# Stacking five chunks of a tile through PE and ACT, field by field, in a DLRM tower kernel

## The chip, the cores and the metric

The kernel runs on one core of one Trainium2 chip. The time is the device time of one execution in microseconds; the figure for a kernel is the median of its runs. The profile is of one further execution, and "the span" is its time from the first to the last instruction.

## The reference

2048 samples have 39 categorical features and 16 dense ones. Each feature f has a table with 1,000 to 125,000 rows of 32 numbers. All 741 pairs of features interact through a 32 x 32 matrix per pair, and a small MLP follows:

```
e = stack([tbl_f[ids[:, f]] for f in range(39)])          # 2048 x 39 x 32
z[b, p] = sum_ac e[b, i, c] * w[a, p, c] * e[b, j, a]      # p runs over pairs i < j
h = relu(concat([z, dense]) @ W_top1 + b_top1)             # 757 -> 512
h = relu(h @ W_top2 + b_top2)                              # 512 -> 256
y = h @ W_top3                                             # 256 -> 1
```

## The kernel before, in words

**Tiles, chunks, units, batches.** The samples are cut into 4 tiles of 512 (`NT`, `NB`). Four features form a chunk g (0 to 9; chunk 9 has three fields), so that 4 x 32 numbers fill the 128 partitions. A unit (g, gi, j) is the product of feature j of chunk g with the up to four features of chunk gi. There are 200 units in a tile, in the order of `UNITS`, which takes the chunks as `PHASES = (0, 1, 2, 3, 7, 4, 8, 5, 6, 9)`. Two units are a step, two steps a batch; a tile is 50 batches. Chunk (t, g) means chunk g of tile t.

**A unit.** `interact` (L578) multiplies on PE the pair matrices (`w4`, stationary) with the stacked form of feature j (`e4`, moving, 512 samples) into one of two buffers of `u_ps`. `multiply` (L907) on DVE multiplies a step of `u_ps` with the transposed embeddings `eT` into `prod`. `reduce` (L604) on PE sums over the 32 numbers into `z_ps`, for the batch before. ACT copies finished tiles of `z_ps` to `zT` (`take_z`, L781). In a batch PE runs, in this order: two calls of `interact`, pieces of the MLP of the tile before, `reduce`, `turn` of a chunk, `look_up`s, and, in tile 0, `make_half`. PE, DVE, ACT, POOL and SP each have a program of their own with a fixed order and wait on semaphores.

**Where the embeddings come from.** POOL gathers rows of large tables with an indirect DMA of 128 rows at a time (L422), 4 for each field; the first 96 gathers, which are tile 0's, wait until the third gather before has landed (`WINDOW`), the later ones until DVE has reached a step (`s_mul`). The buffer `e_rows` holds four chunks. `turn` (L528) transposes a gathered chunk into `t_ps` on PE. Small tables are kept in SBUF in three bf16 parts, and `look_up` (L543) multiplies them with one-hot matrices made by DVE (`one_hot_slice`, L886). `FIRST_TILE` and `OTHER_TILES` give the batches in which a chunk is turned or its slices looked up; a chunk's last such batch is its `COMPLETE` batch.

**From `t_ps` to `e4`.** `take_chunk` (L707) on ACT copies `t_ps` to the high part in `parts` (fp32r) and to `eT`; `split_chunk` (L863) on DVE writes the low part. `e4` wants for each field high and low values in alternating partitions, and every field spread over all 128. Most chunks go through DRAM: SP stores both parts (`store_parts`, L461) and loads them again (`stack_chunk`, L471) into `e4`, two loads of 512 KB. Five chunks of tile 0, those in `MADE`, are stacked by PE instead: `make_half` (L562) multiplies the 32 partitions of a field with `rep`, high and low part accumulated, for two fields into two banks, and `take_half` (L727) on ACT copies both into `e4`. For the last three of them the banks are `m_ps`, which the MLP uses from tile 1 on, and the second bank of `z_ps`. `e4` has four slots (`E4_SLOT`); `parts` has two buffers.

**Weights.** In tile 0 the pair matrices are split as well, in 13 preparations k of 16 units: ACT loads them (`load_weights`), casts the high part (`weights_high`, L747), DVE subtracts (`weights_low`, L871), ACT stores both (`weights_rest`), and SP brings pieces to `w4` (`bring_piece`). `PREPS` gives the batch of preparation k: 4 to 12 are in batches 6, 9, 13, 17, 21, 25, 29, 33 and 37. In a batch's program on ACT `weights_high` stands behind `take_z`, `take_chunk` and `take_half`; on DVE `weights_low` stands behind the one-hots.

**First uses in tile 0.** Chunk 4 is first used in batch 14, chunk 8 in the middle of batch 19, chunk 5 in batch 28, chunk 6 in batch 36, chunk 9 in batch 42. They are complete in batches 7, 13, 19, 28 and 31.

Of the kernel before, what the change touches and what calls it, by code (L numbers as in the profile page):

```python
# [5 lines left out]
P = 128  # L6
F = 39
D = 32
# [13 lines left out]
def fields_in(g):  # L22
    return min(C, F - C * g)
# [101 lines left out]
E4_SLOT = {0: 0, 1: 2, 2: 3, 3: 1, 7: 2, 8: 3, 4: 0, 5: 1, 6: 0, 9: 1}  # L125
# [25 lines left out]

MADE = ((0, 1), (0, 0), (0, 2), (0, 3), (0, 7))
MADE_FIRST = 2
MADE_IN = {1: (((0, 2), 0), ((0, 2), 1)), 4: (((0, 3), 0), ((0, 3), 1)), 5: (((0, 7), 0),), 6: (((0, 7), 1),)}
MLP_WEIGHTS_BATCH = 7
LATE = (17, 39)
# [8 lines left out]
ORDER = [(0, g) for g in BEGIN] + [(t + nxt, g) for t in range(NT) for g, nxt, turn, slices in chunks_of_tile(t)]  # L165
POS = {c: n for n, c in enumerate(ORDER)}
# [22 lines left out]

def stores_to(n):  # L190

    return len([m for m in range(n + 1) if (m - n) % 2 == 0 and ORDER[m] not in MADE])


def halves_before(c, half):
# [5 lines left out]
def e4_before(c):  # L201

    t, g = c
    same = [x for x in PHASES if E4_SLOT[x] == E4_SLOT[g]]
    n = same.index(g)
    return (t, same[n - 1]) if n else (t - 1, same[-1]) if t else None


def e4_loads(c):

    same = [x for x in PHASES if E4_SLOT[x] == E4_SLOT[c[1]]]
    return len(same) * c[0] + same.index(c[1]) + 1
# [5 lines left out]
for t in range(NT):  # L218
    for g, nxt, turn, slices in chunks_of_tile(t):
        c = (t + nxt, g)  # L220
# [9 lines left out]
    INDICES.setdefault(LAST_SLICE.get(LOOKED[LPOS[c] - 2], -1) + 1, []).append(c)  # L230
for b, cs in COMPLETE.items():
    for c in cs:
        if c in MADE:
            continue
        x = e4_before(c)
        free = NBAT * x[0] + J_LAST[x[1]] // UPB + 1 if x else 0

        late = LATE[0] <= b < LATE[1]
        STORES.setdefault(b + 1 + late, []).append(c)
        STACKS.setdefault(max(b + (4 if late else 3 if b < LATE[0] else 2), free), []).append(c)  # L240
# [43 lines left out]
def tower(nc, tables, ids, hot_ids, hot_rows, dense, w, w1, b1, w2, b2, w3, sel_in, ident_in, y):  # L284
# [4 lines left out]
    with ExitStack() as ctx:  # L289
# [9 lines left out]
        parts = sb("parts", [P, 2, 2, NB], F32R)  # L299
        e4 = sb("e4", [P, ES, C, NB], F32R)  # L300
# [98 lines left out]
        def step_after(t, g):  # L399

            return NS * t + J_LAST[g] // UPS + 1
# [117 lines left out]
        def _(pe):  # L519
# [42 lines left out]
            def make_half(c, half):  # L562
# [12 lines left out]
                                                start=h == 0, stop=h == 1)  # L575
                last.then_inc(s_stk, 1)

            def interact(t, n):  # L578
                s = NS * t + n
                if s >= 2:  # L580
                    pe.wait_ge(s_mul, s - 1)
                slots = [e_slot(t, UNITS[UPS * n + i][1]) for i in range(UPS)]
                for i in range(UPS):
                    u = UPS * n + i
                    g, gi, j = UNITS[u]
                    if u == J_FIRST[g]:
                        pe.wait_ge(s_e4[E4_SLOT[g]], 32 * e4_loads((t, g)))
                    if u % PW == 0:
                        p = NPW * t + u // PW
                        pe.wait_ge(s_w4[p % WR], 16 * (p // WR + 1))  # L590
                    place = i if slots[0] <= slots[1] else 1 - i
                    p = NPW * t + u // PW
                    last = nc.tensor.matmul(u_ps[:, s % 2, place, :], w4[:, p % WR, (u % PW) * P:(u % PW + 1) * P],  # L593
                                            e4[:, E4_SLOT[g], j - C * g, :], start=True, stop=True)
                last.then_inc(s_u, 1)
# [86 lines left out]
            for t in range(NT):  # L682
                for b in range(NBAT):
                    for x in range(SPB):
                        interact(t, SPB * b + x)
                    if t:
                        for piece in mlp_pieces(b, t == NT - 1):
                            mlp_piece(t - 1, *piece)
                    if b:
                        reduce(t, b - 1)  # L690
                    elif t:
                        reduce(t - 1, NBAT - 1)
                    for c in TURNS.get(NBAT * t + b, ()):
                        turn(c)
                    for c, k in TAKES.get(NBAT * t + b, ()):
                        look_up(c, k)
                    if t == 0:
                        for c, half in MADE_IN.get(b, ()):
                            make_half(c, half)
                    if t == NT - 1:  # L700
                        for m, k in EARLY.get(b, ()):
                            early_piece(t, m, k)
# [3 lines left out]
        def _(act):  # L706
            def take_chunk(c):  # L707
                t, g = c
                n = POS[c]
                rows = D * fields_in(g)  # L710
                if n >= 2:
                    if ORDER[n - 2] in MADE:
                        act.wait_ge(s_stk, 2 * MADE.index(ORDER[n - 2]) + 2)
                    else:
                        act.wait_ge(s_scr[n % 2], 32 * stores_to(n - 2))
                if hot(c):
                    act.wait_ge(s_look, LOOK_BEFORE[c] + slices_of(g))
                else:
                    act.wait_ge(s_tp, GPOS[c] + 1)
                nc.scalar.copy(parts[0:rows, n % 2, 0, :], t_ps[0:rows, :]).then_inc(s_eh, 1)  # L720

                before = t - 2 if g in TWO_PLACES else t - 1
                if before >= 0:
                    act.wait_ge(s_mul, NS * (before + 1))
                nc.scalar.copy(eT[0:rows, e_slot(t, g), :], t_ps[0:rows, :]).then_inc(s_et, 1)  # L725

            def take_half(c, half):  # L727
                made = MADE.index(c)
                act.wait_ge(s_stk, 2 * made + half + 1)
                x = e4_before(c)  # L730
                if x:
                    act.wait_ge(s_u, step_after(*x))
                slot, q = E4_SLOT[c[1]], UPS * half
                if made < MADE_FIRST:
                    nc.scalar.copy(e4[:, slot, q:q + UPS, :], u_ps[:, half, :, :]).then_inc(s_e4[slot], 16)
                else:
                    nc.scalar.copy(e4[:, slot, q, :], m_ps[:, :]).then_inc(s_e4[slot], 8)
                    nc.scalar.copy(e4[:, slot, q + 1, :], z_ps[:, 1, :]).then_inc(s_e4[slot], 8)

            def load_weights(k):  # L740
                a, b = PREP_UNITS[k]
# [44 lines left out]
            def take_mlp(t, layer, m, src):  # L786
                act.wait_ge(s_m, NI * t + ITEM[layer, m] + 1)
                if layer == 1:
                    if m == 0 and t > 0:
                        act.wait_ge(s_y, 16 * t)  # L790
                    nc.scalar.activation(h1[:, m, :], src, ACT.Relu, bias=b1s[:, m:m + 1]).then_inc(s_mc, 1)  # L791
                elif layer == 2:
                    nc.scalar.activation(h2[:, t % 2, m, :], src, ACT.Relu, bias=b2s[:, m:m + 1]).then_inc(s_mc, 1)
                else:
                    nc.scalar.copy(y_sb, src[0:1, :]).then_inc(s_mc, 1)
                    act.wait_ge(s_mc, NI * (t + 1))
                    act.dma_start(y[t:t + 1, :], y_sb).then_inc(s_y, 16)
# [30 lines left out]
            for t in range(NT):  # L828
                for b in range(NBAT):
                    if t:  # L830
                        for layer, m, k in mlp_pieces(b, t == NT - 1):
                            if k == LAYER_INPUTS[layer] - 1:
                                take_mlp(t - 1, layer, m, m_ps[:, :])
                    for tile in range(NZ):
                        done = ends_tile(tile) // UPB + 1
                        if done == b:
                            take_z(t, tile)
                        elif t and done == NBAT and b == 0:
                            take_z(t - 1, tile)
                    for c in COMPLETE.get(NBAT * t + b, ()):  # L840
                        take_chunk(c)
                    if t == 0:
                        for c, half in MADE_IN.get(b, ()):
                            take_half(c, half)
                        if b == LAST_TABLE_BATCH:
                            table_high(HOT_CHUNKS[-1])
                        if b == LAST_TABLE_BATCH + 2:
                            table_middle(HOT_CHUNKS[-1])
                        if b - 1 in PREPS:
                            weights_rest(PREPS[b - 1])  # L850
                        if b in PREPS:
                            weights_high(PREPS[b])
                        if b in PREP_LOADS:
                            load_weights(PREP_LOADS[b])
# [171 lines left out]
```

## Time and profile before

| | |
|---|---|
| median of 3 runs | 739.4 us (738.17 to 740.45) |
| profiled execution | 739.08 us |
| its span | 737.2 us, mean granted TensorE clock 0.977 |
| PE busy | 678.2 us |
| DVE busy | 608.3 us |
| POOL busy | 415.6 us |
| ACT busy | 104.3 us |
| moved by DMA | 141.40 MB |

The engines' busy times overlap in time. PEld are PE's weight loads. In timelines a row is a run of like instructions: its start in us from the span's start, its length in us, engine, line, operation, tiles and shapes, count, and in brackets the idle time of the engine before it with what ended it. A name with a q (SPq, ACTq) is the engine's queue, which issues DMAs.

### The profile page before, as it was taken

What the parts mean: (1) busy time and instruction counts of PE and PEld (TensorE: products, weight loads), DVE (VectorE), ACT (ScalarE), POOL (GpSimd) and SP (SyncE); (2) the same over time, 40 slices, a digit from 0 to 9 for tenths busy, and PEclk for the clock granted to TensorE, in tenths of its full rate; (3) what the DMA queues carried; (4) which work ended last, traced back from release to release, by engine and by line L of the source; (5) the groups of instructions that cost most, each with busy time, mean ns of one, the idle gap of its engine ahead of it and who ended that gap; (6) DMA issues with size and microseconds to landing.
All of it is one profiled execution on the core that took longest, in us unless ns stands there. A gap on an engine that the chain in (4) does not pass through costs nothing.

```text
span 737.2 us, 10924 instructions
## 1 busy us (share of the span) xinstructions
PE 678.2 (92%) x4202; PEld 274.6 (37%) x4202; DVE 608.3 (83%) x773; ACT 104.3 (14%) x186; POOL 415.6 (56%) x424
## 2 busy tenths in 40 slices
PE   0678886898997999999999999999999999999998
PEld 0233332333333444434344444433434444343443
DVE  3776797799996998898889997998889978788740
ACT  3423301111110010101211010110110101011002
POOL 5777465567777766567766665567766666000000
PEclk9888999899998999999999999999999999999999
DMA  7644979779876573547675582728686373553200
GB/s 200 209 119 138 334 272 301 252 231 314 284 227 202 195 257 108 166 140 236 224 225 192 202 281 68 240 85 259 194 270 214 125 254 98 179 174 104 97 0 0
DMA packets 72271, 141.40 MB, mean 192 GB/s; under 512 B 13829, under 2 KB 23704, under 8 KB 72092
## 3 DMA queue, kind: packets, MB, share of 16 engines
q1 hardware_dynamic: 48796, 116.86, 46.2%
q10 hardware_dynamic: 9984, 16.94, 6.4%
q0 software_dynamic: 13440, 6.91, 6.4%
q8 instruction: 33, 0.54, 0.3%
q14 instruction: 18, 0.15, 0.1%
HBM read 109.66 MB, written 31.00 MB: 191 GB/s over the span
## 4 chain that ended last, share of the span: by engine, by line
PE 70%; DVE 14%; issue 7%; DMA 4%; POOL 3%; ACT 1%; SPq 0%; DVEq 0%; ACTq 0%
PE u_ps L593 23%; PE z_ps L617 21%; DVE prod L914 9%; PE m_ps L630 8%; PE t_ps L556 7%; DVE one_hot L902 4%; POOL e_rows L422 3%; PE m_ps L632 3%; PE t_ps L537 2%; DMA e<-scratch 1%; DMA e_rows<-in_tbl_dram,idx 1%; PE u_ps L652 1%; PE u_ps L661 1%; PE m_ps L634 1%; PE t_ps L644 1%
## 5 line engine op out<-in xcount | busy, mean ns | idle before, releaser
L422 POOL DMA_INDIRECT e_rows<-in_tbl_dram,idx x420 | 415.4, 989 | 212.9 <-issue 89.9
L914 DVE TENSOR_TENSOR prod<-u_ps,eT 128x1024 f32<-128x1024 f32 x400 | 469.5, 1216 | 77.6 <-PE u_ps L593 77.1
L593 PE MATMUL u_ps<-e,w 128*128 128x512 f32 x800 | 260.9, 437 | 24.6 <-DVE prod L914 14.6
L617 PE MATMUL z_ps<-prod,sel 128*32 128x512 f32 x1600 | 222.9, 614 | 0.0
L593 PEld LDWEIGHTS u_ps<-e,w 128*128 128x128 f32 x800 | 132.2, 190 | 173.4 <-DVE prod L914 85.9
L902 DVE TENSOR_SCALAR one_hot<-hot_idx,row 125x512 bf16<-125x512 f16 (+2 forms) x296 | 107.6, 420 | 9.6 <-PE t_ps L556 5.8
L556 PE MATMUL t_ps<-one_hot,tb 125*32 125x512 bf16 x1344 | 104.2, 392 | 10.5 <-DVE one_hot L902 9.1
L556 PEld LDWEIGHTS t_ps<-one_hot,tb 125*32 125x32 bf16 x1344 | 43.7, 99 | 89.3 <-issue 57.6
L617 PEld LDWEIGHTS z_ps<-prod,sel 128*32 128x32 f32 x1600 | 33.8, 108 | 111.7 <-issue 87.4
L630 PE MATMUL m_ps<-zT,w1s 128*128 128x512 f32 x144 | 73.5, 592 | 0.0
L720 ACT CAST parts<-t_ps 128x512 fp32r<-128x512 f32 (+1 forms) x40 | 23.4, 586 | 295.4 <-PE t_ps L556 162.4
L868 DVE TENSOR_TENSOR parts<-eT,parts 128x512 fp32r<-128x512 f32 (+1 forms) x40 | 27.3, 683 | 3.2 <-ACT eT L725 3.2
L630 PEld LDWEIGHTS m_ps<-zT,w1s 128*128 128x128 f32 x144 | 27.2, 189 | 6.4
L791 ACT ACTIVATE h<-m_ps,b1s 128x512 f32<-128x512 f32 x13 | 9.0, 689 | 145.1 <-PE m_ps L630 143.9
L784 ACT COPY zT<-z_ps 128x512 f32<-128x512 f32 x24 | 14.1, 586 | 102.9 <-PE z_ps L617 102.9
L537 PE MATMUL t_ps<-ident,e_rows 128*128 128x128 f32 (+2 forms) x112 | 19.2, 296 | 6.6 <-DMA e_rows<-in_tbl_dram,idx 6.6
L632 PE MATMUL m_ps<-h,w2s 128*128 128x512 f32 x48 | 24.5, 592 | 0.0
L725 ACT COPY eT<-t_ps 128x512 f32<-128x512 f32 (+1 forms) x40 | 23.7, 591 | 0.0
L537 PEld LDWEIGHTS t_ps<-ident,e_rows 128*128 128x128 f32 (+2 forms) x112 | 12.2, 142 | 30.3 <-issue 27.1
L875 DVE TENSOR_TENSOR h<-h 128x512 fp32r<-128x512 f32 (+1 forms) x13 | 8.7, 668 | 2.7 <-ACT h L751 2.7
L751 ACT CAST h<-h 128x512 fp32r<-128x512 f32 (+1 forms) x13 | 7.9, 609 | 17.2 <-DMA h<-in_w_dram 17.2
L632 PEld LDWEIGHTS m_ps<-h,w2s 128*128 128x128 f32 x48 | 9.0, 188 | 2.1
(52 smaller groups left out, 122.2 us busy)
## 6 DMA issues: line engine op xcount, KB each, us to landing
w<-w_rows SPq DMA_DIRECT2D x100, 512.0 KB
e<-scratch SPq DMA_DIRECT2D x62, 512.0 KB, 5.7
scratch<-parts SPq DMA_DIRECT2D x62, 256.0 KB
w_rows<-h ACTq DMA_DIRECT2D x48, 256.0 KB
e_rows<-in_tbl_dram,idx POOLq DMA_INDIRECT x420
hot_idx<-hot SPq DMA_DIRECT2D x12, 512.0 KB
h<-in_w_dram ACTq DMA_DIRECT2D x12, 256.0 KB, 4.3
e<-scratch SPq DMA_DIRECT2D x8, 384.0 KB
```

Source lines behind the costliest of these rows:

```text
L422: pool.indirect_dma_start(e_rows[:, r, n, D * q:D * q + D], None, tables[f], bass.IndirectOffsetOnAxis(ap=idx[:, t, f * TPG + n:f * TPG + ...
L537: last = nc.tensor.transpose(t_ps[0:hi, b * P:b * P + P], rows, ident[:, :])
L556: last = nc.tensor.matmul(t_ps[D * q:D * q + D, :], tb[0:HP, part, col:col + D], one_hot[0:HP, n % OS, here * NB:(here + 1) * NB], start=k ...
L593: last = nc.tensor.matmul(u_ps[:, s % 2, place, :], w4[:, p % WR, (u % PW) * P:(u % PW + 1) * P], e4[:, E4_SLOT[g], j - C * g, :], start=T ...
L617: last = nc.tensor.matmul(z_ps[D * quad:D * quad + D, z % 2, :], sel[:, D - 1 - row:2 * D - 1 - row], prod[:, (NS * t + n) % PR, place, :] ...
L630: last = nc.tensor.matmul(m_ps[:, :], w1s[:, k, m * P:m * P + P], zT[:, t % 2, k, :], start=k == 0, stop=stop)
L632: last = nc.tensor.matmul(m_ps[:, :], w2s[:, k, m * P:m * P + P], h1[:, k, :], start=k == 0, stop=stop)
L720: nc.scalar.copy(parts[0:rows, n % 2, 0, :], t_ps[0:rows, :]).then_inc(s_eh, 1)
L725: nc.scalar.copy(eT[0:rows, e_slot(t, g), :], t_ps[0:rows, :]).then_inc(s_et, 1)
L868: nc.vector.tensor_tensor(parts[0:rows, n % 2, 1, :], eT[0:rows, e_slot(t, g), :], parts[0:rows, n % 2, 0, :].bitcast(F32), ALU.subtract). ...
L902: last = nc.vector.tensor_scalar(one_hot[0:HP, n % OS, i * NB:(i + run) * NB], hot_idx[0:HP, LPOS[c] % 2, x * NB:(x + run) * NB], (row10 i ...
L914: nc.vector.tensor_tensor(prod[:, s % PR, :, :], u_ps[:, s % 2, :, :], e, ALU.mult).then_inc(s_mul, 1)
```

## The change

Chunks 4, 8, 5, 6 and 9 of tile 0 are no longer stored and loaded. `FIELD_WISE` gives each its first batch. At the end of PE's batch `first + q` `make_field` multiplies field q's high and low part (two matmuls, accumulated) into the one bank `m_ps`, and `take_field` on ACT copies it into `e4`. `take_field` stands in ACT's batch ahead of `take_z`, `take_chunk` and the weights. A field's matmuls wait until the field before has been copied out of `m_ps`. `take_chunk` waits for the last field that was made from its buffer of `parts`, in place of a store.

```diff
+FIELD_WISE = {(0, 4): 9, (0, 8): 15, (0, 5): 21, (0, 6): 30, (0, 9): 35}
+STACKED = MADE + tuple(FIELD_WISE)
...
-    return len([m for m in range(n + 1) if (m - n) % 2 == 0 and ORDER[m] not in MADE])
+    return len([m for m in range(n + 1) if (m - n) % 2 == 0 and ORDER[m] not in STACKED])
+
+
+def stk_at(c, part):
+
+    earlier = STACKED[:STACKED.index(c)]
+    return sum(2 if x in MADE else fields_in(x[1]) for x in earlier) + part + 1
+
+
+def stk_after(c):
+    return stk_at(c, (2 if c in MADE else fields_in(c[1])) - 1)
+
+
+def field_in(b):
+
+    return [(c, b - first) for c, first in FIELD_WISE.items() if first <= b < first + fields_in(c[1])]
...
-        if c in MADE:
+        if c in STACKED:
             continue
...
+            def make_field(c, q):
+
+                n = POS[c]
+                pe.wait_ge(s_el, n + 1)
+                d = c if q else STACKED[STACKED.index(c) - 1]
+                pe.wait_ge(s_e4[E4_SLOT[d[1]]], 32 * e4_loads(d) - (32 - 8 * q if q else 0))
+                own = slice(D * q, D * q + D)
+                for h in range(2):
+                    last = nc.tensor.matmul(m_ps[:, :], rep[own, 2 - 2 * h:2 - 2 * h + P], parts[own, n % 2, h, :],
+                                            start=h == 0, stop=h == 1)
+                last.then_inc(s_stk, 1)
...
+                    if t == 0:
+                        for c, q in field_in(b):
+                            make_field(c, q)
...
-                    if ORDER[n - 2] in MADE:
-                        act.wait_ge(s_stk, 2 * MADE.index(ORDER[n - 2]) + 2)
+                    if ORDER[n - 2] in STACKED:
+                        act.wait_ge(s_stk, stk_after(ORDER[n - 2]))
...
+            def take_field(c, q):
+                act.wait_ge(s_stk, stk_at(c, q))
+                act.wait_ge(s_u, step_after(*e4_before(c)))
+                slot = E4_SLOT[c[1]]
+                rest = 8 if q < fields_in(c[1]) - 1 else 32 - 8 * q
+                nc.scalar.copy(e4[:, slot, q, :], m_ps[:, :]).then_inc(s_e4[slot], rest)
...
+                    if t == 0:
+                        for c, q in field_in(b):
+                            take_field(c, q)
                     for tile in range(NZ):
```

## Rows read from the trace of the kernel before

**Rows 1.** The page's busy line: us, share of the span, instructions.

```profile
PE 678.2 (92%) x4202; PEld 274.6 (37%) x4202; DVE 608.3 (83%) x773; ACT 104.3 (14%) x186; POOL 415.6 (56%) x424
```

**Rows 2.** Waits of PE from 70 to 300 us: total, times, longest.

```profile
PE u_ps L593 <- DVE prod L914: 12.1, 29, 1.3
PE u_ps L593 <- DMA e<-scratch: 5.8, 1, 5.8
PE t_ps L537 <- DMA e_rows<-in_tbl_dram,idx: 4.1, 1, 4.1
```

**Rows 3.** Timeline of PE around batch 19.

```profile
131.03 1.19 PE L593 MATMUL u_ps<-e,w 128*128 128x512 f32 x2 [5.76 <-DMA e<-scratch]
...
134.50 1.18 PE L593 MATMUL u_ps<-e,w 128*128 128x512 f32 x4
```

**Rows 4.** The chain that ended last, 60 to 300 us: start, us, what.

```profile
115.66 3.91 DMA scratch<-parts
...
120.27 10.62 DMA e<-scratch
```

**Rows 5.** Timeline of PE at `make_half`; tile `e`, its copies on ACT (min/median/max ns).

```profile
81.98 0.50 PE L574 MATMUL m_ps<-parts,rep 32*128 32x512 f32 x1
...
82.65 1.19 PE L593 MATMUL u_ps<-e,w 128*128 128x512 f32 x4
...
L737 ACT CAST e<-m_ps x4: 585/586/587, 72.6 to 82.8; 128x512 fp32r<-128x512 f32 x4
```

**Rows 6.** Timelines of ACT, PE and DVE, batches 16 to 19.

```profile
116.64 0.62 ACT L751 CAST h<-h 128x512 fp32r<-128x512 f32 x1 [4.60 <-DMA h<-in_w_dram]
...
120.88 1.06 PE L617 MATMUL z_ps<-prod,sel 128*32 128x512 f32 x8
...
122.66 0.68 DVE L875 TENSOR_TENSOR h<-h 128x512 fp32r<-128x512 f32 x1
...
123.26 3.48 DVE L914 TENSOR_TENSOR prod<-u_ps,eT 128x1024 f32<-128x1024 f32 x3
```

**Rows 7.** Timeline of DVE behind batch 13.

```profile
112.08 0.69 DVE L875 TENSOR_TENSOR h<-h 128x512 fp32r<-128x512 f32 x1 [1.22 <-ACT h L751]
```

**Rows 8.** Timelines of PE and DVE, start of batch 25.

```profile
151.76 1.61 PE L593 MATMUL u_ps<-e,w 128*128 128x512 f32 x4
...
154.52 2.34 DVE L914 TENSOR_TENSOR prod<-u_ps,eT 128x1024 f32<-128x1024 f32 x2
```

**Rows 9.** Timelines of DVE, ACT and PE, batch 33 and batches 37 and 38.

```profile
183.23 0.68 DVE L875 TENSOR_TENSOR h<-h 128x512 fp32r<-128x512 f32 x1
...
194.89 0.58 ACT L784 COPY zT<-z_ps 128x512 f32<-128x512 f32 x1 [19.06 <-PE z_ps L617]
195.37 0.41 ACT L751 CAST h<-h 128x256 fp32r<-128x256 f32 x1
195.41 1.20 PE L593 MATMUL u_ps<-e,w 128*128 128x512 f32 x4
...
195.81 0.43 DVE L875 TENSOR_TENSOR h<-h 128x256 fp32r<-128x256 f32 x1
```

**Rows 10.** Timelines of POOL and PE, batches 48 to 50.

```profile
221.44 0.73 PE L593 MATMUL u_ps<-e,w 128*128 128x512 f32 x2
...
221.96 0.94 POOL L422 DMA_INDIRECT e_rows<-in_tbl_dram,idx  x1 [0.30 <-issue]
...
228.96 2.05 PE L593 MATMUL u_ps<-e,w 128*128 128x512 f32 x4
...
232.81 1.35 PE L593 MATMUL u_ps<-e,w 128*128 128x512 f32 x4
```

**Rows 11.** POOL's waits from 87.6 to 160 us; two stretches (PE, PEld, DVE, ACT, POOL busy; clock; DMA share, GB/s).

```profile
POOL e_rows L422 <- DMA e_rows<-in_tbl_dram,idx: 26.5, 18, 3.2
...
107.00:117.00 10.00, 8.12 (x49) 2.76 (x47) 8.78 (x11) 1.95 (x4) 7.86 (x8) 1.00 0.50 155
117.00:127.00 10.00, 7.67 (x38) 2.38 (x38) 9.52 (x9) 0.26 (x1) 4.10 (x5) 1.00 1.01 322
```

More of the change, by code:

```diff
@@ L728, in take_half @@
                 made = MADE.index(c)
-                act.wait_ge(s_stk, 2 * made + half + 1)
+                act.wait_ge(s_stk, stk_at(c, half))
                 x = e4_before(c)
```

## The prediction

> **What bounds the kernel now.** I read the busy line of the page first [rows 1]: PE is busy for 92% of the span and DVE for 83%, ACT for 14%. Work added to ACT is nearly free, work added to PE or DVE may not be. Then I read what PE waits for between 70 and 300 us [rows 2]: one wait of 5.8 us for the load of `e` from scratch, and one of 4.1 us for gathered rows. Nearly everything else it waits for is DVE, in pieces up to 1.3 us. The change takes away the first wait and may touch the second; both lie in tile 0. A batch is two calls of `interact` (2 x 2 matmuls of L593), so the n-th batch starts at matmul 4n of L593; I counted batches that way in the timeline.
>
> The timeline of PE shows the first wait [rows 3]. It is in the middle of batch 19, at the first unit of chunk 8: after 5.76 us without work the next matmuls start at 131.03. The chain of waits shows the two transfers that the change removes for this chunk, 3.91 us of store and 10.62 us of load [rows 4].
>
> **What it removes.** Without the load the second pair of batch 19 waits for the product before it. The three products in a row from 123.26 us [rows 6] take 1.16 us each; the second ends at 125.6. So the pair starts at 125.6 and not at 131.03, 5.4 us earlier. After the wait PE ran slow: from 131.03 to batch 20 at 134.50 is 3.47 us [rows 3], and in the same work at full clock a pair is 0.7, `reduce` 1.0 and `turn` 0.4, with gaps 2.3 us. That is 1.2 us more. Batch 20 would start at 127.9: **6.6 us** earlier, before anything is paid.
>
> The other four chunks cost PE no wait today; removing their 4 stores and loads gains nothing by itself on PE. All five together are 5 x 0.5 MB stored and 5 x 1 MB loaded less on the DMA engines (0.75 of it for chunk 9).
>
> **What it adds.** 19 fields (4+4+4+4+3), each two matmuls on PE and one copy on ACT. The nearest row is `make_half`, which issues four such matmuls: from its start at 81.98 to the next `interact` at 82.65 are 0.67 us [rows 5]. Its four run two on two, the pairs on different row groups and banks. A field's two have one row group and one bank, one after the other, so a field costs as long as a half: 0.65 us. Bounds: 0.34 (half of that, if a neighbour overlaps it), and 1.0 where the clock is low. The 19 fields are 12.4 us of PE. The copy is 0.59 us of ACT [rows 5], 11 us in all, on an engine with 633 us idle.
>
> The Trainium skill (TensorEngine Tiling (Array Packing), Key Properties and Gotcha 1: PSUM Pressure) says that tiles in different row groups run in parallel and need different PSUM banks. It speaks against stacking field by field through one bank: packed in pairs the 19 fields would be 6.3 us of PE, unpacked they are 12.4. The two-on-two starts in the trace agree with it.
>
> How much lies on the path differs by batch, so I laid the fields into the timeline chunk by chunk, moving each instruction to what it waits for.
>
> Chunk 4 (batches 9 to 12): batches 9 to 12 have two slices of look-ups each, so DVE makes one-hots between its products and is the later engine. Only the last field pushes the look-ups of batch 13, whose end already releases ACT and through it a waiting `weights_low` (1.22 us, [rows 7]). Cost 0.5 us; bounds 0 and 1.3.
>
> Chunk 8 (batches 15 to 18): lean batches without one-hots, where PE and DVE take turns. `reduce` of batch 17 starts at 120.88 [rows 6] and the next `interact` follows it at once. The field goes there. In batch 16 it delays the next product by 0.6 us net. In batch 17 there is more: `weights_high(7)` is behind `take_field` in ACT's program, and ran far ahead before (done at 117.3, [rows 6]). Now it waits for the field: PE's field ends about 1.7 us after `reduce` starts, copy 0.6, cast 0.6, and `weights_low(7)`, which DVE reached at 122.66 [rows 6], waits some 1.4 us. That is the wait [rows 7] shows for `take_chunk`. Behind it stand all DVE products, and PE behind these; on ACT the stores of the split weights and the next raw load stand behind the copies too, and SP's pieces of `w4` behind those, but what is prepared in batch 17 is first used in batch 28, so these have some 30 us to spare. SP only loses waits: its pieces of `w4` stood behind stores and stacks, and are paced by `s_u` anyway. Sum for chunk 8: 2.5 us; bounds 1.0 and 4.3. The last field is copied about 0.6 us before the second pair of batch 19 needs it.
>
> So batch 20 starts at 127.9 + 0.5 + 2.5 = 130.9 and not 134.50: 3.6 us earlier.
>
> Chunk 5 (batches 21 to 24): a field ends the batch while DVE makes the next one-hots. After batch 24 PE could start at 151.76, DVE wants its result at 154.52 [rows 8]; 0.65 us more disappears. Cost 0, bounds 0 and 1.3. If that cover were gone it would be 2.6.
>
> Chunks 6 and 9 (batches 30 to 33, 35 to 37): PE has waits for DVE to spare up to batch 31 and few after. In batch 33 `weights_high(11)` is behind `take_field`; with the look-ups before it the cast ends near 184.3, DVE wants it at 183.23 [rows 9]: 1.1 us. Batches 35 and 36 each have look-ups and a field: PE becomes the later one, 0.7 us. In batch 37 the field ends at 195.41 + 0.65 if nothing is late; then `take_field`, `take_z` (0.58) and `weights_high(12)` (0.41) follow in ACT's order, before `weights_low(12)`, which ran at 195.81 [rows 9]. That is 1.7 us, partly the same lateness. Sum **3.5 us**; bounds 1.9 (PE work added less its slack there) and 6.5.
>
> The main line therefore reaches batch 40 with 6.6 - 0.5 - 2.5 - 0 - 3.5 = 0.1 us gained: about as before.
>
> **The second wait.** At the end of batch 48 `turn` of chunk (1, 3) waits 4.1 us [rows 2] for its last gather, which POOL runs at 221.96 and which lands six us later [rows 10]. The clock then falls: batch 48 takes 7.5 us (221.44 to 228.96) where 3.1 would do, batch 49 takes 3.85 (to 232.81) where 2.5 would. Together 4.4 + 1.35 = **5.8 us**. Why is that gather late? POOL issues one every 1.25 us without rest from 160 us on, so its lateness is from before. The first 96 gathers wait each for the landing of the third before, and from 87.6 us, where the first removed store has just been issued, to 160 us such waits are 26.5 us in 18 pieces, 21 us above the ordinary 0.3 us [rows 11]; the first of them (3.2 us) still belongs to loads issued before, so 18 us stand to be changed. Where the DMA engines are half idle (107 to 117, share 0.50) POOL does not wait; at share 1.01 (117 to 127) it does, 5.6 us [rows 11]. Chunks 4, 8 and 5 store and load 4.5 MB in this time, and the two stretches shown move 1.6 and 3.2 MB in 10 us each; at their mean rate of 0.24 MB per us the 72 us hold 17 MB, so a quarter of the traffic goes, in bursts. I take 8 us of them as gone; bounds 2 and 13. With the main line at its old time, 4.1 us suffice to end the wait. From batch 50 on PE runs without idle time to the end (in steady tiles only DVE waits), so what is gained here stays.
>
> **Sum.** Against the profiled execution's 739.1 us (span 737.2 and 1.9 around it): 0.1 + 5.8 = 5.9 us less, 733.2. The median of the runs is 0.3 us above that execution: 733.5 us.
>
> **Rivals.**
> A. *The gather stays late.* The first wait moves to the second: main line gains, turn (1, 3) waits until 228 as before. It speaks for it that POOL is at its rate of 1.25 us from 160 us on, so nothing later can make up; against it that its waits follow the DMA share. POOL earlier by 0 to 2 us gives 737 to 739.4, no change.
> The Trainium skill (DMA: Bandwidth & Descriptors, Queues, rings and completion order) says that each DMA engine takes turns between its queues by packets. By that rule a gather is slowed by other queues having work at all, not by how much, and a shorter queue of SP helps only where it runs empty; the quiet stretch at share 0.50 fits it as well. Its time is that of A.
> B. *The fields are cheap.* DVE hides most of them, as its full stretches suggest: main line costs 3 us in place of 6.5, gain 3.6 there, and POOL early by over 8 us: 729.9. If POOL is only 6 earlier, 732.
> C. *PE becomes the bound from batch 9 to 37*, the other side. All 19 fields on the path at 0.65 are 12.4 us, and the casts behind `take_field` add 1.4 + 1.1 + 1.7 = 4.2. Against 6.6 + 5.8 gained: 4.2 us slower, 743.6. It decides from 12.4 us of cost on, that is from every field paid in full. Against it: PE has 12.1 us of waits for DVE between 70 and 300 us [rows 2], most of them in these batches, and half of the fields lie in batches with one-hots.
> D. *The change does nothing for the first wait*, since the last field of chunk 8 is taken late by ACT: needs ACT blocked by a weight load for over 3 us in batches 17 and 18. These loads are now issued later too, but four batches ahead of use. 737.
>
> **How the numbers follow.** About 0.3% (2.2 us) is what a measurement of this kernel can tell from none. Forecast (gain 3 to 8 us, around 733.5) 0.55; A 0.15, of which a third at the edge counts as faster; B 0.16; C 0.10; D 0.04. Faster by over 0.3%: 0.55 + 0.16 + 0.05 = 0.76, less 0.02 for sizes: 0.74. Within: 0.10 + 0.04 = 0.15 with these. Slower: 0.11. The range leaves out C and the far end of B: low 729.0 (B with its bound), high 739.5 (A at nothing).
>
> **What would show it.** In the profile after: no wait of PE for `e<-scratch` in tile 0; make_field's matmuls 0.33 us apart and its copies 0.59 us; batch 20 near 131 us at full clock; waits of DVE for ACT's L751 cast in batches 17, 33 and 37, of 1 to 2 us; batch 40 near 200 us as before; POOL's waits for landings between 87.6 and 160 us about 18 us in place of 26.5; no wait of `turn` near 222 us and the clock at 1.00 from 80 us on. I am wrong if POOL is not earlier (batch 49 still starts near 229), or if PE's batches 15 to 37 grow by over 0.6 us each.

## The result and the profile after

The changed kernel takes 736.1 us, median of 20 runs (730.32 to 739.01), against 738.29 us (734.78 to 741.08) for the kernel before in 20 runs on the same chip. The ratio is 0.9957 [0.9937, 0.9976], that is 3.2 us less [1.8, 4.7]. The two medians alone differ by 2.2 us; the ratio is taken over all the runs, and gains are given by it below. The forecast was 5.9 us less. The sign and the range hold, the size is about half.

One thing was misread, in the description of the change as well as in the prediction: the fields do not stand at the end of PE's batch. In the changed kernel the call of `make_field` stands right behind the two `interact`s, ahead of the MLP's pieces, `reduce`, `turn` and `look_up`. Experiment e4 below builds the place that was assumed.

The page of the changed kernel, its busy line (us, share of the span, instructions) and what the queues moved; its span is 734.3 us, the execution 736.1 us, the mean granted clock 0.977:

```profile
PE 690.1 (94%) x4240; PEld 282.0 (38%) x4240; DVE 608.0 (83%) x773; ACT 115.1 (16%) x205; POOL 414.0 (56%) x424
...
DMA packets 68304, 133.94 MB, mean 182 GB/s; under 512 B 13509, under 2 KB 23384, under 8 KB 68124
```

Against [rows 1]: 38 more matmuls and 19 more copies, 11.9 us more of PE and 10.8 of ACT, 7.5 MB less. PE's share grew by two points and the kernel still got faster.

The waits of PE from 70 to 300 us (total, times, longest), to be read against [rows 2], then those of POOL from 87.6 to 160 us, against [rows 11], and of DVE from 70 to 230 us:

```profile
PE u_ps L623 <- DVE prod L957: 7.7, 17, 1.5
PE m_ps L592 <- ACT e L771: 1.3, 1, 1.3
...
POOL e_rows L440 <- DMA e_rows<-in_tbl_dram,idx: 14.1, 12, 2.8
...
DVE h L918 <- ACT h L791: 5.4, 4, 2.9
```

The waits for `e<-scratch` (5.8 us) and for gathered rows (4.1 us) are both gone. POOL's landing waits fell from 26.5 to 14.1 us. Neither gives its full length at the end, as the starts of the batches show (us from the span's start):

| batch | 5 | 7 | 9 | 15 | 20 | 25 | 40 | 50 | 54 | span |
|---|---|---|---|---|---|---|---|---|---|---|
| before | 74.5 | 82.6 | 89.8 | 114.0 | 134.5 | 151.8 | 200.3 | 232.8 | 247.0 | 737.2 |
| after | 73.8 | 84.4 | 91.5 | 116.1 | 135.1 | 153.8 | 202.4 | 228.6 | 244.1 | 734.3 |

Read by stages the change loses 2.5 us between batches 5 and 7, ahead of its first new instruction, and 0.4 between 9 and 15; it gains only 1.6 between 15 and 20, loses 1.4 between 20 and 25 and 0.1 between 25 and 40, gains 6.2 between 40 and 50 and gives 1.2 back by batch 54. With batch 5 starting 0.7 earlier that is the 2.9 us between the two spans. Behind batch 54 both take 490.2 us.

Timeline of PE and DVE in the changed kernel where `e<-scratch` was waited for before (start, length, engine, line, ..., idle before and its end):

```profile
114.25 0.69 DVE L918 TENSOR_TENSOR h<-h 128x512 fp32r<-128x512 f32 x1 [1.43 <-ACT h L791]
...
116.13 0.73 PE L623 MATMUL u_ps<-e,w 128*128 128x512 f32 x2 [1.48 <-DVE prod L957]
117.26 0.73 PE L623 MATMUL u_ps<-e,w 128*128 128x512 f32 x2 [0.40 <-DVE prod L957]
117.92 1.04 PE L604 MATMUL m_ps<-parts,rep 32*128 32x512 f32 x2
118.90 1.93 PE L647 MATMUL z_ps<-prod,sel 128*32 128x512 f32 x8
120.77 2.08 PE L623 MATMUL u_ps<-e,w 128*128 128x512 f32 x4
...
132.49 1.25 PE L623 MATMUL u_ps<-e,w 128*128 128x512 f32 x4
...
135.08 1.09 PE L623 MATMUL u_ps<-e,w 128*128 128x512 f32 x3
```

Batch 19 starts at 132.49 and runs on into batch 20 without the wait. But the same four matmuls that take 1.25 us at 132.49 take 2.08 at 120.77, and `reduce` 1.93 in place of 1.06: from 118.1 to 128.4 us the granted clock is 0.50, the lower level (1.2 GHz). It came 2 us behind a PE wait of 1.48 us for DVE, which had itself waited 1.43 us for a cast on ACT.

And the end of batch 48, against [rows 10]. `turn` of chunk (1, 3) stands at 226.13 with no wait, batch 49 follows at 226.54, batch 50 at 228.65:

```profile
225.14 1.06 PE L647 MATMUL z_ps<-prod,sel 128*32 128x512 f32 x8
226.13 0.66 PE L555 MATMUL t_ps<-ident,e_rows 128*128 128x128 f32 x4
226.54 1.18 PE L623 MATMUL u_ps<-e,w 128*128 128x512 f32 x4
227.65 1.06 PE L647 MATMUL z_ps<-prod,sel 128*32 128x512 f32 x8
228.65 0.73 PE L623 MATMUL u_ps<-e,w 128*128 128x512 f32 x2
```

Its last gather on POOL, at 221.96 before [rows 10]:

```profile
215.34 0.94 POOL L440 DMA_INDIRECT e_rows<-in_tbl_dram,idx  x1 [0.30 <-issue]
```

### The profile page after: what moved, and what is told of

Same layout as the page of the kernel before. It is cut to its first block, busy times and chain, and to the rows that moved or that the text cites. A ratio compares the mean times of both kernels' runs of the same rounds, so it can differ in the third digit from the quotient of the medians.

```text
span 734.3 us, 11032 instructions
## 1 busy us (share of the span) xinstructions
PE 690.1 (94%) x4240; PEld 282.0 (38%) x4240; DVE 608.0 (83%) x773; ACT 115.1 (16%) x205; POOL 414.0 (56%) x424
## 4 chain that ended last, share of the span: by engine, by line
PE 77%; DVE 12%; issue 6%; POOL 2%; ACT 1%; DMA 1%; DVEq 0%; ACTq 0%
PE u_ps L623 26%; PE z_ps L647 23%; PE m_ps L660 8%; DVE prod L957 8%; PE t_ps L574 8%; DVE one_hot L945 3%; PE m_ps L662 3%; POOL e_rows L440 2%; PE t_ps L555 2%; PE m_ps L604 1%; PE u_ps L682 1%; PE u_ps L691 1%; PE m_ps L664 1%; PE t_ps L674 1%; PE m_ps L674 1%
## 5 line engine op out<-in xcount | busy, mean ns | idle before, releaser
L623 PE MATMUL u_ps<-e,w 128*128 128x512 f32 x800 | 260.3, 438 | 13.8 <-DVE prod L957 10.2
L824 ACT COPY zT<-z_ps 128x512 f32<-128x512 f32 x24 | 14.1, 586 | 79.8 <-PE z_ps L647 79.8
L778 ACT CAST e<-m_ps 128x512 fp32r<-128x512 f32 x19 | 11.1, 586 | 64.8 <-PE m_ps L604 64.0
L604 PE MATMUL m_ps<-parts,rep 32*128 32x512 f32 x38 | 14.9, 472 | 0.0
```

## The experiments

The times are medians of 12 runs (9 for e7, 7 for e9), and each ratio is against runs of the kernel before on the same chip. All starts of batches, waits and clocks are of one profile for each run; the last table puts the main ones together.

### e1 and e2: only chunk 8, all but chunk 8

```diff
-FIELD_WISE = {(0, 4): 9, (0, 8): 15, (0, 5): 21, (0, 6): 30, (0, 9): 35}
+FIELD_WISE = {(0, 8): 15}                                                  (e1)
+FIELD_WISE = {(0, 4): 9, (0, 5): 21, (0, 6): 30, (0, 9): 35}               (e2)
```

> Only chunk 8 goes through m_ps field by field; chunks 4, 5, 6 and 9 of tile 0 are stored and loaded as before. Theory 1 (first wait ended by chunk 8 alone, second wait ended by POOL being earlier through less DMA traffic): PE has no wait for e<-scratch in batch 19; POOL's waits for landings between 87.6 and 160 us lie between those of before (26.5) and after (14.1), near 21, so the first gather of chunk (1, 2) goes out near 155 us and the last of chunk (1, 3) near 218; with the cost of 15 fields saved the main line is up to 4 us earlier at batch 48 and turn of chunk (1, 3) waits again, 2 to 6 us. Time 1 to 3 us below before. Rival (the traffic doesn't matter, only chunk 8's wait): the same time as the changed kernel or lower, with no wait at batch 48.

> Chunks 4, 5, 6 and 9 field by field, chunk 8 stored and loaded as before. Theory 1: the wait of PE for e<-scratch in batch 19 is back, 3 to 6 us, with the low clock behind it; POOL's waits for landings between 87.6 and 160 us near 19 us and its last gather of chunk (1, 3) early enough, so no wait at batch 48, as the main line is late. Time 0 to 3 us below before. Rival (all of the gain is the first wait): the same as before within 1 us.

Measured: e1 736.0 us, ratio 0.997 [0.9947, 0.9993]; e2 735.34 us, ratio 0.996 [0.9941, 0.9979]. Waits of PE and of POOL (same stretches as above) in e1:

```profile
PE t_ps L555 <- DMA e_rows<-in_tbl_dram,idx: 4.6, 2, 4.2
...
POOL e_rows L440 <- DMA e_rows<-in_tbl_dram,idx: 22.7, 16, 3.1
```

and in e2:

```profile
PE u_ps L623 <- DMA e<-scratch: 3.1, 1, 3.1
...
POOL e_rows L440 <- DMA e_rows<-in_tbl_dram,idx: 18.6, 13, 2.8
```

In these two profiles each half of the change ends one of the two waits and leaves the other. With chunk 8 alone batch 40 comes at 198.1, 2.2 us earlier than before, and the gathered rows take it back (4.2 us at `turn`): the first wait alone is a loan. With the other four, POOL is early enough and the second wait is gone. By the ratios the halves gain 2.2 us [0.5, 3.9] and 3.0 us [1.5, 4.4], both together 3.2 [1.8, 4.7]. The gains seem not to add, but the intervals are too wide to show it.

### e3: the changed kernel with the removed traffic put back

Fields and copies stay as changed. SP also stores `eT` to scratch and loads scratch into an unused half of `zT`, in the sizes and at the places of the removed stores and loads (2.5 MB and 5 MB); ACT waits for these loads once, before tile 1's first `take_z`. Nobody in tile 0 waits for them.

```diff
                     for c in STACKS.get(NBAT * t + b, ()):
                         stack_chunk(c)
+                    for c in ALSO_STACKS.get(NBAT * t + b, ()):
+                        stack_also(c)
```

> The changed kernel, and beside it SP issues stores and loads of the same sizes and at the same places of its queue as before (eT to scratch, scratch to zT's second half), which nobody waits for but the copies of tile 1. Theory 1: POOL's waits for landings between 87.6 and 160 us are back at 24 to 28 us, its last gather of chunk (1, 3) at 219 to 223 us, and turn of chunk (1, 3) waits 2 to 5 us at batch 48: 2 to 4 us above the changed kernel. Rival (POOL was early for another reason than the bytes): POOL's waits stay near 14 us and the time is that of the changed kernel.

Measured: 738.13 us, ratio 1.0008 [0.9988, 1.0028]. Waits of POOL, and the timeline of PE at the end of batch 48:

```profile
POOL e_rows L452 <- DMA e_rows<-in_tbl_dram,idx: 26.8, 17, 3.7
```

```profile
226.66 1.09 PE L590 MATMUL t_ps<-ident,e_rows 128*128 128x128 f32 x4 [5.01 <-DMA e_rows<-in_tbl_dram,idx]
227.40 2.05 PE L658 MATMUL u_ps<-e,w 128*128 128x512 f32 x4
```

Landing waits of 26.8 us against 26.5 before and 14.1 in the changed kernel, the 144th gather at 223.3, the wait of `turn` back at 5.0 us with the low clock behind it, and the whole gain gone: its interval and the changed kernel's don't overlap. The early gather comes from the removed traffic. Rival A (the gather stays late whatever the traffic) falls. Whether it is the bytes or the mere presence of SP's transfers that slows the gathers, this edit doesn't tell, as it puts back both. The main line, with all fields and without the first wait, reaches batch 40 at 197.8 here, 2.5 us earlier than before; the wait of `turn` takes it back, as in e1.

### e4: the fields at the end of PE's batch

```diff
                         interact(t, SPB * b + x)
-                    if t == 0:
-                        for c, q in field_in(b):
-                            make_field(c, q)
...
                             make_half(c, half)
+                    if t == 0:
+                        for c, q in field_in(b):
+                            make_field(c, q)
```

> The changed kernel with make_field at the end of PE's batch, behind reduce, turn and look_up, which is where my working placed it; the change has it right behind interact. Theory 1 (the place decides what ACT and through it DVE's weights_low wait for): DVE waits for the L-line of weights_high in batches 17, 33 and 37, 1 to 2 us each, where the changed kernel has 0.6, 0 and 0.4; batches 15 to 38 take 1.5 to 3 us longer in all at full clock, and the time is 1 to 3 us above the changed kernel. Rival (fields cost PE time only, wherever they stand): the same stage table and time as the changed kernel.

Measured: 737.03 us, ratio 0.9979 [0.9956, 1.0002]. The timeline of ACT and DVE in batch 37 of e4:

```profile
194.98 0.59 ACT L778 CAST e<-m_ps 128x512 fp32r<-128x512 f32 x1 [2.83 <-PE m_ps L604]
195.46 0.59 ACT L824 COPY zT<-z_ps 128x512 f32<-128x512 f32 x1
195.94 0.42 ACT L791 CAST h<-h 128x256 fp32r<-128x256 f32 x1
...
196.39 0.42 DVE L918 TENSOR_TENSOR h<-h 128x256 fp32r<-128x256 f32 x1 [1.58 <-ACT h L791]
```

The copy of the field, `take_z` and the cast follow one another without a gap and DVE waits 1.58 us: the chain that the prediction priced at 1.7 us. In the changed kernel the same row stands at 197.87 and waits 0.42:

```profile
197.43 0.41 ACT L791 CAST h<-h 128x256 fp32r<-128x256 f32 x1
197.87 1.18 ACTq L794 DMA_DIRECT2D w_rows<-h  x2
...
197.87 0.43 DVE L918 TENSOR_TENSOR h<-h 128x256 fp32r<-128x256 f32 x1 [0.42 <-ACT h L791]
```

The two kernels' times can't be told apart (the intervals of the ratios overlap), but the stages can. From batch 20 to 40 e4 takes 69.2 us, before 65.8, the changed kernel 67.3. So 3.4 us for the assumed place, where 3.5 were forecast, and 1.5 for the real one. (Within it the split was off: 1.1 us in batches 20 to 25 and 2.3 after, forecast 0 and 3.5.)

### Further profiles of both kernels

The kernels are unchanged; each has two further profiles, each of one execution.

> The kernel before once more, for a second profiled execution. Theory 1: the waits at batch 19 (4 to 7 us) and batch 48 (2 to 6 us) are in every execution, and PE's clock falls behind each. If the fall of the clock near 118 us, which the changed kernel and all four variants show and the first profile of before does not, comes with the change, it is missing here too; if it is the luck of one execution, it can be here.

> The changed kernel once more. Theory 1: no wait at batches 19 and 48; POOL's waits from 87.6 to 160 us 12 to 16 us. The low clock near 118 us is there again, 3.4 to 10.3 us long; rival: it is gone, and the kernel is then 3 us shorter.

> The kernel before a third time. The low clock that begins near 75 us, ahead of every changed instruction, lasted 3.4 us in its first two profiles and 10.2 us in those of the changed kernel. If that is luck of the execution, either length can come here; if something of the program sets it, 3.4 again.

> The changed kernel a third time, for the same question: 10.2 us again near 75 us if the program sets it, either if it is luck. Batches 9 to 50 as in its first two profiles, no wait at batches 19 and 48.

Measured: before 737.46 and 733.89 us, after 734.83 and 736.43 us. The third profile of the kernel before is the one that matters. Its 144th gather, and PE at the end of batch 48:

```profile
219.34 0.94 POOL L422 DMA_INDIRECT e_rows<-in_tbl_dram,idx  x1 [0.30 <-issue]
```

```profile
221.31 0.73 PE L593 MATMUL u_ps<-e,w 128*128 128x512 f32 x2
222.23 0.73 PE L593 MATMUL u_ps<-e,w 128*128 128x512 f32 x2 [0.19 <-DVE prod L914]
222.90 1.06 PE L617 MATMUL z_ps<-prod,sel 128*32 128x512 f32 x8
223.89 0.66 PE L537 MATMUL t_ps<-ident,e_rows 128*128 128x128 f32 x4
```

There is no wait. The gather runs 2.6 us earlier than in [rows 10] (landing waits of 22.7 us, not 26.5), and that is enough. The kernel before has the second wait in some of its executions only (4.1 and 4.7 us in two profiles, none in the third); the changed kernel has it in none of three, its 144th gather standing at 214.1 to 215.7. Batches 40 to 50 of before take 32.5, 33.2 and 26.3 us, of after 26.3 each time. The first wait is there each time, 5.8, 2.5 and 5.1 us. The second profile of before has one more wait for gathered rows, 3.8 us in batch 7, which its other two don't have.

The low clock near 118 us varies too: 10.2, 3.4 and 10.2 us in the three profiles of after, and in before none, 3.4 (from 115.2) and none.

### e6: each field made with four matmuls

The two matmuls of a field are issued twice into the same bank; 38 more matmuls, no more copies.

```diff
-                for h in range(2):
+                for h in (0, 1, 0, 1):
```

> The changed kernel with each field's two matmuls issued twice, the second time over the first: 38 matmuls more. Theory 1 (a field is about 0.65 us of PE, of which part lies under waits for DVE, most of all where DVE has one-hots): 19 further fields of PE work are 8 to 12 us of busy time, and the batches 9 to 40 take 5 to 10 us longer, as the slack is used up by the first 19. Time 5 to 10 us above the changed kernel. Rival (DVE sets the pace in tile 0): at most 2 us longer.

Measured: 741.32 us, ratio 1.0053 [1.0034, 1.0071]: that is 0.96% of before's time, 7.1 us, more than the changed kernel, for 19 x 0.66 = 12.5 us of PE. Part of the 7.1 us is the clock, though: at one and the same mean granted clock, 0.979, five runs of e6 take 739.0 to 741.0 us and two of the changed kernel 734.6 and 735.6, about 5 us less. In batches 20 to 40 2.9 to 3.1 us of the 7.3 added arrive (70.4 us against 67.3 to 67.5). So a second set of fields is not on the path in full, against rival C. It is the price of the second set, which finds part of the slack used; in the same batches the first set cost 1.5 us.

### e7, e8 and e9: the cast ahead of the field's copy

Each low-clock stretch near 118 us lay behind a PE wait of 1.3 to 1.5 us at batch 15 (eight of the eleven profiles with that wait have one), and that behind DVE's wait for `weights_high`, which ACT runs behind `take_chunk` and `take_field`. e7 moves that cast to the front of ACT's batch. e8 makes the same move in the kernel before; e9 is e7 with the fields at the end of PE's batch.

```diff
+                    if t == 0 and b in PREPS:
+                        weights_high(PREPS[b])
                     if t == 0:
                         for c, q in field_in(b):
                             take_field(c, q)
...
-                        if b in PREPS:
-                            weights_high(PREPS[b])
```

> The changed kernel with weights_high of a batch ahead of everything else of that batch in ACT's program, ahead of take_field, take_z and take_chunk. Theory 1 (DVE's weights_low waits for ACT's cast, which stands behind copies that wait for PE): DVE's waits for that cast in batches 7, 14, 18 and 38 (2.9, 1.4, 0.6 and 0.4 us in the changed kernel) go, PE's wait of 1.5 us for DVE at batch 15 with them, and perhaps the low clock near 118 us that follows it; 2 to 5 us less than the changed kernel. Rival (these waits are covered, as PE or POOL sets the pace): within 1 us of it, or the gain is given back by a wait for gathered rows at batch 48.

> The kernel before with weights_high of a batch ahead of everything else of that batch in ACT's program, all chunks stacked as before. Theory 1 (the two waits, batch 19's load and batch 48's gather, take up what an earlier main line gains): DVE's waits for the cast in batches 7 and 14 (1.4 and 1.2 us) go, and PE waits that much longer for e<-scratch at batch 19 or for the gather at batch 48; within 1.5 us of before. Rival (the order alone is worth what it was worth on the changed kernel): 5 to 7 us below before.

> The changed kernel with both edits: weights_high first in ACT's batch, and make_field at the end of PE's batch. Theory 1 (the end of the batch is dearer only since ACT's cast stands behind take_field): with the cast ahead, the place costs little; batches 25 to 40 take 49 us or less, as with the cast first alone (48.8), and the time is within 1.5 us of that kernel's 730.0. Rival (the place itself is dear on PE): batches 25 to 40 near 50.8 us as with the fields at the end alone, and 2 us or more above 730.0.

Measured: e7 729.99 us, ratio 0.9915 [0.9887, 0.9943]; e8 737.39 us, ratio 0.9991 [0.9967, 1.0015]; e9 732.14 us, ratio 0.9904 [0.987, 0.9938]. e7 and e9 beat the kernel before by 6.3 and 7.1 us by their ratios. e7's interval lies below the changed kernel's altogether but for an overlap of 0.0006.

In e7 DVE no longer waits for the cast, PE doesn't wait at batch 15, and the clock stays up. The same DVE row as in the timeline of the changed kernel (114.25), and batch 15:

```profile
110.37 0.68 DVE L918 TENSOR_TENSOR h<-h 128x512 fp32r<-128x512 f32 x1
...
112.24 0.73 PE L623 MATMUL u_ps<-e,w 128*128 128x512 f32 x2
```

Windows from 118.1 to 128.4 us (length; busy us and instructions of PE, PEld, DVE, ACT, POOL; granted clock, DMA share, GB/s), first the changed kernel, then e7:

```profile
118.10:128.40 10.30, 10.30 (x30) 3.86 (x30) 5.68 (x6) 1.17 (x2) 6.39 (x8) 0.50 0.41 121
```

```profile
118.10:128.40 10.30, 10.30 (x62) 4.14 (x58) 9.46 (x12) 2.94 (x6) 7.08 (x8) 1.00 0.73 225
```

PE is busy the whole stretch in both, with 30 matmuls in one and 62 in the other. A busy share alone would not show this loss.

In e8 the main line gains as well, but the two waits stand where they stood and take it:

```profile
PE t_ps L537 <- DMA e_rows<-in_tbl_dram,idx: 5.5, 2, 5.2
PE u_ps L593 <- DMA e<-scratch: 2.4, 1, 2.4
```

Batch 40 comes at 195.5 and batch 50 at 228.3 nevertheless. This suggests that the reordering and the change are worth more together, as what the one gains on PE is no longer lost at a DMA wait. The times don't show it: e8's 0.7 us [-1.1, 2.4] and the change's 3.2 [1.8, 4.7] make 3.9, and e7's 6.3 has the interval [4.2, 8.3]. e9 is a reason for care: in its profile `turn` still waits 4.0 us for gathered rows (144th gather at 218.5), yet its ratio is e7's within the noise. Its median is 2.1 us above e7's, just past the 2 us named as the rival's sign, but on another chip and with few runs, so the times settle nothing. The stages do: with the cast ahead, batches 20 to 40 take 67.1 us there, not e4's 69.2, and batches 25 to 40 take 48.8, as forecast. The end of the batch was dear through the cast.

| kernel | 9 to 15 | 15 to 20 | low clock near 118 or 130 | 20 to 40 | 40 to 50 | 144th gather | landing waits |
|---|---|---|---|---|---|---|---|
| before | 24.2 | 20.5 | 6.8 | 65.8 | 32.5 | 222.0 | 26.5 |
| before, again | 22.3 | 18.3 | 6.8 | 65.8 | 33.2 | 221.7 | 25.9 |
| before, third | 24.2 | 20.1 | 6.8 | 65.7 | 26.3 | 219.3 | 22.7 |
| after | 24.6 | 19.0 | 10.2 | 67.3 | 26.3 | 215.3 | 14.1 |
| after, again | 24.8 | 15.9 | 3.4 | 67.4 | 26.3 | 214.1 | 15.4 |
| after, third | 25.1 | 19.0 | 10.2 | 67.5 | 26.3 | 215.7 | 16.3 |
| e3 | 24.6 | 16.0 | 3.4 | 67.5 | 32.6 | 223.3 | 26.8 |
| e7 | 22.7 | 14.4 | 0 | 67.4 | 26.3 | 213.2 | 11.9 |
| e8 | 23.2 | 16.1 | 3.4 | 66.2 | 32.8 | 220.3 | 24.4 |
| e9 | 22.7 | 14.8 | 0 | 67.1 | 31.8 | 218.5 | 20.4 |

## Why the prediction was right in sign and too large

**The first wait (term of 6.6 us): the mechanism is right, its size varies.** There is no `e<-scratch` wait in tile 0 in any profile of the changed kernel; rival D falls. The wait was 5.8, 2.5 and 5.1 us in three profiles of before, and the term was made from the longest.

**Chunk 4 and chunk 8 (0.5 and 2.5 us): right as work, with one thing unforeseen.** Batches 9 to 15 grew by 0.4 us. From batch 15 to 20 the forecast leaves 16.4 us (114.5 to 130.9); 15.9 were measured with 3.4 us of low clock, 19.0 with 10.2. The recorded sum for chunk 8 is also larger than what it names: 0.6 and 1.4 us make 2.0, not 2.5. Batch 20 came at 135.1 and not at 130.9. Of the 4.2 us between, 1.8 were there at batch 7 and 2.6 came in this stretch. That the clock stays at 1.00 from 80 us on was wrong. That the stretch is tied to the PE wait at batch 15 is shown as far as e7, e8 and e9 go, one profile each, where both are gone; e6 had the wait (1.5 us) and no fall, as had two profiles of before (1.3 us), so the wait doesn't settle it. The wait for the cast in batch 13, [rows 7], was in the prediction, but only as a cover for a cost.

**The other 1.8 us** are from batches 5 to 7: 10.6 us where before took 8.2, with 10.2 us of low clock in place of 3.4, all ahead of the first field. Before (three profiles) and e3 have 3.4 us there, all other kernels 10.2, e8 among them, which has no field at all. In all 14 profiles the stretch before it, near 55 us, goes with it: 6.8 us there with 3.4 here, or 3.4 there with 10.2 here. So neither the fields nor the removed traffic sets it, and what does stays open.

**Chunk 5 (nothing) and chunks 6 and 9 (3.5 us): the step that failed by place.** The working took the fields to be last in PE's batch. For that place it was nearly right in total (e4: 3.4). In the changed kernel the field is ready one `reduce` and its look-ups earlier, `take_field` and the cast behind it move up, and the wait in batch 37 is 0.42 us; of the predicted waits of 1 to 2 us in batches 17, 33 and 37 there are 0.60, none and 0.42. Chunks 6 and 9 cost 0.1 us, chunk 5 about 1.4, of which 0.5 appear in e1 too (17.8 us from batch 20 to 25 against 17.3), where chunk 5 has no field. Of itself this error made the forecast gain 2 us too small. By stages all 19 fields cost about 3.9 us or less, an estimate: 0.4, 1.5, and for chunk 8 at most 2.0 (15.9 us with some low clock in it, less the 13.9 that the forecast leaves without these fields; e7 takes 14.4). The forecast booked 6.5, so on the fields alone rival B's 3 us was the nearer price, and the longer low clock near 75 and 118 us, which no term held, took that gain away.

**The second wait (5.8 us): the step whose size failed.** The path was right: less traffic, landing waits down (by 12.4 us, 8 forecast within 2 to 13), POOL 6.6 us earlier at the 144th gather, no wait; e3 shows it. Two things make it worth less. Batches 50 to 54 take 14.2 us in before's two profiles with the wait and 15.4 in the third and in the changed kernel, so 1.2 us come back and 5.0 to 5.6 us net are left. And the term holds only for executions in which before has the wait at all, two profiles of three. One execution was taken for the kernel; two more of before would have shown that the first wait varies from 2.5 to 5.8 us and that the second comes and goes. How often the wait stands in the 20 timed runs was not measured, so its mean share in the 3.2 us isn't settled. The three profiled spans of each kernel differ by only 1.0 us in the mean (735.0 and 734.0), the timed runs by more; both are well under 5.9. The mean granted clock, on record for each of the changed kernel's 20 runs, says where the spread comes from: the time follows it almost alone, from 739.0 us at 0.972 to 730.3 and 730.5 at 0.986, and the five runs at 0.977 lie within 0.7 us. Thirteen runs of the kernel before at 0.977, on the chip of e1 to e4, spread over 5.6 us (735.5 to 741.0), about the size of a DMA wait that comes and goes. That the waits are the cause is argued, not shown, as these runs were not profiled.

**The field itself.** Two matmuls in 0.73 us, the copy in 0.59, as priced; at low clock 1.04 to 1.22 us, the upper bound of 1.0 slightly passed.

The Trainium skill, DMA: Bandwidth & Descriptors (Queues, rings and completion order), has each DMA engine take turns between its queues, packet by packet. Read as rival A this would have left the gathers late. The landing waits of e3 and of the changed kernel (26.8 and 14.1 us) decide against that reading, though not against the rule, under which a queue that runs empty also lets the gathers through.

The Trainium skill, TensorEngine Tiling (Array Packing), Key Properties, has tiles work independently and in parallel. It was cited against the change; no run here packs the fields in pairs, so whether that would be faster is not shown.

## What to carry to other kernels

Ask of a removed transfer not only who waited for it but what else it slowed: here slowed gathers made PE wait some 100 us later, for about as long as the wait nearest the change. Take several profiles before a wait of some 5 us is booked as a gain, since one that is marginal stands in some executions only. When work is added to a nearly idle engine, list what a third engine awaits behind it in program order, and put that first, here 6.3 us together with the change (e7), against 3.2 for the change alone, and nothing measurable without it (e8).

## What the runs showed of the hardware

- Gathers land later beside other queues' traffic: 7.5 MB more from SP, with nothing else changed in what POOL does, took its landing waits between 87.6 and 160 us from 14.1 to 26.8 us.
- A PE wait of 1.3 to 1.5 us was followed, 1.3 to 2.6 us later, by a granted clock of 0.50 in some executions and not in others of the same kernel (after: 10.2, 3.4 and 10.2 us of it; before: none, 3.4 and none; e4: 6.8). The long stretch costs about 3 us more than the short one (19.0 and 15.9 us from batch 15 to 20).
- The changed kernel's spread from run to run, 730.3 to 739.0 us, follows the mean granted clock (0.986 to 0.972).
- The same kernel's landing waits vary by 4 us between executions (26.5, 25.9, 22.7); PE's wait of 4 to 5 us further on was there with the first two and not with the third.
